# Two conditioning pieces moved together in a state-space mixer: both behind the convolution taps

## The reference

```python
decay = exp(-exp(w)) * (0.5 + 0.5 * tf)          # one value per batch and channel
a_t = a_{t-1} * decay + ek_t * v_t               # forward and in reverse: nf, nb
b_t = b_{t-1} * decay + ek_t                     # forward and in reverse: df, db
num = nf + nb - ekv + euk * v
den = df + db - ek + euk
out = sigmoid(r) * (num / max(den, 1e-8)) * (0.8 + 0.2 * tf)
x = x + mixer(cond(x));  x = x + moe(cond2(x));  ...
```

```python
hBC = silu(conv(hBC) + conv_b);  xs, B, C = split(hBC)
h = exp(dt * A) * h + (dt * x) B^T;  y = h C + D * x
g = y * silu(gate);  out = (g * rsqrt(mean(g * g) + eps) * norm_w) @ W_out.T
```

## Time and profile before

| what | value |
|---|---|
| median of 3 runs | 1377.38 us (1377.21 to 1378.56) |
| the profiled execution | 1379.72 us, of which the span of the program is 1377.70 us |
| TensorE busy | 1183.8 us, 86% of the span |
| VectorE busy | 852.5 us, 62% |
| ScalarE busy | 599.4 us, 44% |
| GpSimd busy | 441.1 us, 32% |
| mean granted TensorE clock | 0.951 of full speed |
| the mixer | from about 55 us to about 410 us of the span |

### The profile page before, as it was taken

How to read it: one execution, slowest core, us unless ns; L and a number is a source line. 1 busy time by engine, 2 the same in 40 slices (tenths; PEclk the granted TensorE clock), 3 DMA queues, 4 the chain that set the end, 5 groups by cost and what they waited for, 6 DMA issues and landing times. The chain is left out here.

```text
span 1377.7 us, 16485 instructions
## 1 busy us (share of the span) xinstructions
PE 1183.8 (86%) x4614; PEld 627.1 (46%) x4614; DVE 852.5 (62%) x1308; ACT 599.4 (44%) x1747; POOL 441.1 (32%) x467
## 2 busy tenths in 40 slices
PE   0379997799958999999969989887998879987998
PEld 0134443344424444444345546433874338743443
DVE  7799995999965543455249677488531794314232
ACT  4345554555543222322246566476751766601110
POOL 0425664256650000000007447266530574400000
PEclk9999999999987999999989999898998989988999
DMA  6000000000033000000030000300000000000000
GB/s 265 23 1 1 1 1 1 0 0 0 28 119 144 0 0 1 0 0 34 0 152 2 1 0 0 139 7 1 1 1 1 0 0 0 0 8 0 0 0 30
DMA packets 5490, 33.32 MB, mean 24 GB/s; under 512 B 528, under 2 KB 1936, under 8 KB 3536
## 3 DMA queue, kind: packets, MB, share of 16 engines
q1 hardware_dynamic: 5424, 32.61, 6.0%
HBM read 31.56 MB, written 1.05 MB: 24 GB/s over the span
## 5 line engine op out<-in xcount | busy, mean ns | idle before, releaser
L1397 POOL TENSOR_TENSOR prob_latent<-prob_latent,inverse_latent 128x128 f32<-128x128 f32 (+1 forms) x128 | 87.3, 706 | 371.5 <-DVE inverse_latent L1387 371.1
L812 POOL TENSOR_TENSOR decays<-decays,scores 128x768 f32<-128x768 f32 x64 | 125.8, 1969 | 141.3 <-ACT decays L747 141.1
L1987 POOL TENSOR_TENSOR f_pair<-m,weights 128x256 f32<-128x256 f32 x80 | 91.0, 1157 | 95.0 <-DVE m L2008 93.9
L1095 PE MATMUL ph<-h,weights 128*128 x256 | 116.1, 598 | 0.0
L580 PE MATMUL pg<-h,weights 128*128 (+1 forms) x136 | 65.9, 608 | 57.6 <-PEq L359 55.0
L747 ACT ACTIVATE decays<-pcum,neg_cum 128x256 f32<-128x256 f32 (+1 forms) x256 | 86.5, 428 | 6.1 <-PE pcum L633 5.8
L1237 DVE TENSOR_TENSOR mid<-up,ph 128x512 f32<-128x512 f32 x44 | 30.3, 688 | 93.9 <-ACT up L1152 93.9
L1152 ACT ACTIVATE up<-ph 128x512 f32<-128x512 f32 x44 | 26.3, 597 | 140.5 <-PE ph L1095 140.5
L580 PE MATMUL px<-h,weights 128*128 x136 | 71.6, 651 | 15.5 <-DVE conv L880 15.5
L880 DVE SCALAR_TENSOR_TENSOR conv<-px,pp,conv 128x510 f32<-128x510 f32 (+2 forms) x102 | 75.8, 743 | 14.3 <-ACT conv L719 11.8
L674 PE MATMUL pout<-g,weights 128*128 128x512 f32 x128 | 66.7, 646 | 17.3 <-DVE g L935 15.8
(11 more groups left out here) (328 smaller groups left out, 2817.7 us busy)
## 6 DMA issues: line engine op xcount, KB each, us to landing
weights<-in_w_mixer SPq DMA_DIRECT2D x2, 2048.0 KB, 18.8
weights<-in_w_moe SPq DMA_DIRECT2D x2, 1536.0 KB, 7.6
moe_rest<-in_w_moe SPq DMA_DIRECT2D x2, 1536.0 KB, 13.3
weights<-in_w_gqa SPq DMA_DIRECT2D x1, 3072.0 KB, 10.2
weights<-in_w_gqa SPq DMA_DIRECT2D x1, 2048.0 KB, 14.7
weights<-in_w_moe SPq DMA_DIRECT2D x1, 1920.0 KB, 8.5
weights<-in_w_mixer SPq DMA_DIRECT2D x1, 1536.0 KB, 13.1
weights<-in_w_moe SPq DMA_DIRECT2D x1, 1152.0 KB, 12.3
```

The costliest lines, as they stand in the source:

```text
L812: nc.gpsimd.tensor_tensor(decays[:, head % 4], decays[:, head % 4], scores[:], ALU.mult).then_inc(decay_scaled, 1)
L1095: op = nc.tensor.matmul(out[:], wt[:, n * D + k * P:n * D + (k + 1) * P], net.h[:, ds(i * PAIR + k * TOK, TOK)], start=(k == 0), stop=(k = ...
L1397: op = nc.gpsimd.tensor_tensor(self.prob[:, slot, cols], self.prob[:, slot, cols], self.inverse[:, slot, t:t + 1].to_broadcast([P, P * (t ...
L1987: op = nc.gpsimd.tensor_tensor(out[:, :, s, :], src[:, :, 1 - s, :], sin[:, None, s, :].to_broadcast([P, 4, HALF]), ALU.mult)
```

## The change

In the mixer, VectorE took one piece of the conditioning unit behind the taps of a step, and the second one behind take_x, ahead of y and g. Now it takes both directly behind the taps. Neither the number of pieces nor the step in which one is taken is different.

```diff
                     if s >= 2:
-                        take(cond, 1)
+                        take(cond, 2)
                     if s < N:
                         silu_x(i, s + 2)
                         silu_gate(i, s)
                     if 0 <= s - 1 < N:
                         take_x(i, s - 1)
-                    if s >= 2:
-                        take(cond, 1)
                     if 0 <= s - LAG_Y < N:
                         gated(i, s - LAG_Y, link)
```

## The result

The changed kernel took 1356.26 us, the median of four runs (1354.94 to 1356.34), beside 1377.30 us for the kernel before (four runs, 1376.42 to 1378.56). The ratio is 0.9844, with a 95% interval of 0.9827 to 0.9861.

The account below looks back on a forecast made before the run. TensorE and VectorE were both near full, with VectorE made late by waiting for GpSimd. Per pair 7.10 minus 0.30 plus 1.0 gives 7.8 us, 15.6 for two: 1361.8 us forecast, range 1357.5 to 1370.

Parts of the forecast that it names:

- the cause and the bound: In the mixer, VectorE's second piece waits for GpSimd's product; without that wait TensorE becomes the bound.
- The eleven steps: Stretch in the middle of each pair's mixer run, TensorE steps from px to px: 100.05 us to fall to 92.95.
- the exclusion: A VectorE and a GpSimd operation on SBUF exclude each other for their whole length; 1.3 us a scan, 1.64 an addition.
- Rival 2: GpSimd always wins and g lands where it did, behind product and sum; no gain, about 1377 us; chance 0.07.
- the second term: Later silus delay pg in scan steps: 0.30 us of new TensorE waits per pair, between 0 and 1.0.
- rival 3: In scan steps silu_x loses its turn to GpSimd's odd product, holding pg: 5.0 us slower, 1382.4 us; chance 0.07.
- The sign set for it: silu_x above 1 us, or TensorE waits for gate at pg over 1 us in total, would prove the forecast wrong.
- rival 1: The wait moves to g behind GpSimd's even product; addition steps stay at 8.74 us; 8.4 us gain, 1369.0; chance 0.20.
- the floor of 8.45 us: TensorE's own pace per step, read from the step behind the eleven; steps of 8.73 to 10.97 us would fall to it.
- the third term: End of a pair: VectorE brings the last taps forward and g shortens; 1.0 us a pair, bounds 0 and 1.8.
- The part for g: End of a pair: a late g takes 1.81 us against 0.68 undisturbed, so 1.13 us may go.
- The sign set for the tails: TensorE's idle time ahead of pout should fall from 15.5 us to under 4.

Follow-up runs that it names:

- the small product: GpSimd's product cut to 128 by 2 elements, in the kernel before (old order) and in the changed kernel: 1355.27 and 1354.57 us.
- filled tail: Kernel before, with unread TensorE products in idle time at each pair's end: nine per pair 1378.55 us, five per pair 1378.77 us (both 1.0003).
- scan steps alone: Kernel before, with both pieces directly behind the taps only in steps 4, 5, 7 and 8: 1374.27 us (0.9974).

## Why the prediction was right and where it failed

**Right: the cause and the bound.** The eleven steps fell to TensorE's own pace, and the small product shows that the exclusion was what kept them from it. By the middle alone, 15.8 us were won, where 13.6 were forecast (7.10 minus 0.30, twice). In step 8 the course is the one forecast: counted from the taps at 133.02, silu_x starts at 4.48 us (4.49 forecast) and g ends at 8.60 (8.7). Rival 2 is out: g no longer ends where it did, 9.28 us after the taps.

**Right: the second term, and rival 3 in small.** 0.30 us were taken for silus that come late, and 0.32 us were measured in one step of each pair instead of a little in each scan step; with the 0.16 us in the head it is 0.48, inside the bounds of 0 and 1.0. The sign set for it did show: silu_x above 1 us, though once a pair. The mechanism is that of rival 3: GpSimd's odd product is there first, and silu_x waits. As a rival it failed because the scans of the other steps hardly wait for the even product; there silu_x starts 0.29 us ahead of the odd product (137.50 against 137.79), and it is GpSimd that waits: 2.04 us instead of 1.81. The Trainium skill's rule of issue order (SBUF — State Buffer, "Who interferes with whom") is now seen on silu_x too: 2.23 us at 128.21 behind a product issued at 127.76, which agrees.

**Partly right: rival 1.** The even product does come in front of the first addition in steps 10 to 13 (1.93 us for two instead of 1.3), and g does stay long. Neither decides, because a plain step of VectorE has time to spare: no step of 8.74 us is left.

**Wrong, the first step: the floor of 8.45 us.** I took the shortest step of before for TensorE's own pace. That step still had a pout that waited for g, though no idle time stands in its row: g ended at 200.90, and the pout began at 200.94. Before (first fence), and the pout of the same step after (second):

```profile
200.00 0.90 DVE L935 TENSOR_TENSOR g<-y,gate 128x512 f32<-128x512 f32 x1
200.94 1.98 PE L674 MATMUL pout<-g,weights 128*128 128x512 f32 x4
```

```profile
192.32 1.88 PE L674 MATMUL pout<-g,weights 128*128 128x512 f32 x4
```

The group takes 1.98 us where it starts from a wait and 1.88 where it follows on. The pace is 8.35, 0.10 less, 22 times: 2.2 us.

**Wrong, the step that decided: the third term, the end of a pair.** I took 1.0 us a pair with a bound of 1.8; the tails gave 4.38 and 3.72. I priced TensorE's wait at one place (0.67) and a part of g's, and not how far VectorE was behind when the tail begins: 4.97 us from px to taps, against 2.83 once it keeps up. In a step such a delay can cost nothing: in step 9 of the kernel after the taps come 4.38 us behind px (141.54 against 137.16), and TensorE is busy for the whole 8.35 us. In the tail the chain of taps, exponentials, decays, py, y and g runs in the open, so 1.2 us of the delay are paid there. The part for g was priced about right, 1.13 us against the 1.0 by which it got shorter. Lead and g bring 2.1 us in the second pair by the trace, and the kernel with the old placement in the late steps shows that the steps before are enough for it. The rest, 1.6 us in each pair and some 0.7 more in the first, is products at full instead of half clock. The sum had no term for it, although the rows of 3.29 us stood in the trace. The filled tail shows that this local difference is there; its part in the whole time stays open. The sign set for the tails missed with it: the idle time ahead of pout should have fallen under 4 us, and the four waits in the tails still make 7.0.

**Too wide: what excludes what.** The prediction speaks of any operation of VectorE on SBUF. The reciprocal, which has one operand, was not held: 0.96 us at 380.54 beside GpSimd's product of 380.50 to 382.31, 0.94 alone. The bound of den, which has one too, was: 2.06 us at 372.07 beside the product of 372.03 to 373.84, 0.42 alone. All are rows of the kernel before, in its last steps.

Together, 2.2 for the floor and 6.1 for the tails are 8.3 us more than forecast in the profiled executions; the other parts add 0.7, which no run here explains. The medians show 5.4, since the two profiled executions lie 2.4 us above and 1.3 us below theirs, 3.7 us together.

## What to carry to other kernels

Where operations of two engines exclude each other, find out when the other engine is idle in each period, and put the long operations there; here one line for that was worth 21 us of 1377. An engine's delay behind the bound can cost nothing in the steady part and is paid where the pipeline empties (here 1.2 us of 2.14 at the end of a pair): read it as the distance from one engine's event to the next one's, at the last step, and price it there. And take the bound's pace from its products without any wait, not from the shortest step.

## What was not expected of the hardware

- The same wait of 1.60 us in the same place left the products behind it at 1.98 us in one execution and at 3.63, 3.26 and 3.25 in three others (scan steps alone, and both filled tails). Behind waits of 2.73 and 2.78 us they took 3.19 and 3.29, behind 1.87 they took 3.12, behind 1.78 they took 1.98.
- Restoring full clock by products that nobody reads shortened a tail by 1.65 us and the whole time by nothing (1.0003).
- A wait for the other engine stands in the rows as a longer operation and not as idle time: 2.23 us for silu_x instead of 0.67, on a VectorE that is 8.48 us busy in a step of 8.67.
